# Reordering the last of four batches in a fused convolution-attention and channel-attention kernel

## The reference

```python
qkv = concat(x @ wq.T, x @ wk.T, x @ wv.T)                # 768 channels
dw  = depthwise 5x5 convolution of qkv
pw  = grouped 1x1 convolution of dw (groups of 8)
f   = concat(qkv, pw) as 64 heads of (query, key, value), 8 channels each
query, key = relu(query), relu(key)
scores = einsum("bhdn,bhen->bhde", concat(value, ones), key)
out = einsum("bhde,bhen->bhdn", scores, query)
out = out[:, :, :-1] / (out[:, :, -1:] + 1e-15)
x1 = batchnorm(proj @ out) + x
```

```python
norm = (x1 - mean) / sqrt(var + 1e-5)                     # over the positions of a channel
energy = (f_w @ norm + f_b).T @ (g_w @ norm + g_b)        # 1024 x 1024
attention = softmax(energy)
out = o_w @ ((h_w @ x1 + h_b) @ attention.T) + o_b + x1
```

## Time and profile before

| | us |
|---|---|
| median of 3 runs | 700.99 |
| the runs | 698.55, 703.51, 700.99 |
| span of the profiled execution, from its first to its last instruction | 700.8 |
| PE busy | 636.0 (91%) |
| DVE busy | 563.5 (80%) |
| POOL busy | 541.0 (77%) |
| ACT busy | 470.7 (67%) |

### The profile page before, as it was taken

One profiled execution on the slowest core, in us unless ns is written; L12 is line 12 of the kernel. 1 busy time (PEld: TensorE's weight loads), 2 busy tenths in 40 slices (PEclk: granted clock), 3 DMA queues, 4 the chain that ended last, 5 costly groups with the idle time before them and its releaser, 6 DMA issues.

```text
span 700.8 us, 8645 instructions
## 1 busy us (share of the span) xinstructions
PE 636.0 (91%) x3176; PEld 475.3 (68%) x3176; DVE 563.5 (80%) x661; ACT 470.7 (67%) x745; POOL 541.0 (77%) x253
## 2 busy tenths in 40 slices
PE   4979978999989999999989999999898977997998
PEld 3854537665868787656778877648677773485887
DVE  5899899788989999989999998989999993442321
ACT  4787608897777769888676977987886662232231
POOL 4899996999999899999999999999999891000000
PEclk9979999999999999999999999999999998899999
DMA  8000001001010000001100000000100000000000
GB/s 296 2 0 1 0 0 61 1 1 34 27 61 15 16 31 1 0 1 60 61 1 16 16 31 1 1 0 1 61 15 16 9 22 1 0 1 0 16 16 30
DMA packets 6537, 16.23 MB, mean 23 GB/s; under 512 B 864, under 2 KB 992, under 8 KB 5984
## 3 DMA queue, kind: packets, MB, share of 16 engines
q1 hardware_dynamic: 6496, 15.69, 6.3%
HBM read 11.50 MB, written 4.19 MB: 22 GB/s over the span
## 4 chain that ended last, share of the span: by engine, by line
PE 36%; issue 20%; DVE 16%; ACT 15%; POOL 12%; DMA 1%; POOLq 0%; SPq 0%; DVEq 0%; ACTq 0%
DVE ps L1143 9%; PE ps L629 7%; PE ps L605 7%; ACT prod L895 7%; POOL conv L1354 7%; POOL rows L1354 4%; PE ps L538 4%; PE ps L708 3%; DVE small L1280 2%; PE ps L471 2%; PE ps L620 2%; ACT raw L864 1%; PE ps L756 1%; PE ps L475 1%; PE ps L472 1%
## 5 line engine op out<-in xcount | busy, mean ns | idle before, releaser
L1354 POOL TENSOR_TENSOR conv<-conv,prod 128x930 f32<-128x930 f32 (+4 forms) x197 | 432.4, 2238 | 16.0 <-ACT prod L895 13.2
L1143 DVE SCALAR_TENSOR_TENSOR ps<-raw,dw_sb,ps 128x930 f32<-128x930 f32 (+4 forms) x295 | 354.1, 1201 | 7.6
L895 ACT ACTIVATE prod<-raw,dw_sb 128x930 f32<-128x930 f32 (+4 forms) x233 | 250.2, 1123 | 16.6 <-POOL conv L1354 16.6
L629 PE MATMUL ps<-ht,pt 128*128 128x256 f32 x512 | 115.4, 379 | 2.7 <-ACT pt L1050 2.7
L629 PEld LDWEIGHTS ps<-ht,pt 128*128 128x128 f32 x512 | 95.0, 190 | 14.8 <-ACT pt L1050 3.1
L1041 ACT ACTIVATE rows<-ps,small 128x1024 f32<-128x1024 f32 x32 | 35.6, 1113 | 82.2 <-DVE small L1284 82.2
L1354 POOL TENSOR_TENSOR rows<-rows,prod 128x930 f32<-128x930 f32 (+4 forms) x27 | 62.9, 2329 | 9.9 <-ACT prod L895 6.5
L1280 DVE TENSOR_REDUCE small<-ps 128x1 f32<-128x1024 f32 x32 | 39.1, 1220 | 27.9 <-PE ps L605 27.8
L605 PE MATMUL ps<-hi,t_hi 128*128 128x512 f32 x128 | 45.3, 436 | 14.4 <-ACT rows L1041 14.4
L471 PE MATMUL ps<-hi,wqkv_hi 128*128 128x512 f32 x92 | 38.9, 423 | 4.4 <-ACT vt L910 4.4
L605 PE MATMUL ps<-lo,t_hi 128*128 128x512 f32 x128 | 41.2, 404 | 0.0
(11 more groups left out here) (146 smaller groups left out, 1059.3 us busy)
## 6 DMA issues: line engine op xcount, KB each, us to landing
q_raw<-x_dram SPq DMA_DIRECT2D x8, 512.0 KB, 6.2
x<-x_dram SPq DMA_DIRECT2D x4, 1024.0 KB, 4.7
out_dram<-x_t SPq DMA_DIRECT2D x16, 256.0 KB, 2.3
conv<-wqkv_dram SPq DMA_DIRECT2D x1, 768.0 KB, 4.5
conv<-fg_dram SPq DMA_DIRECT2D x1, 512.0 KB, 5.1
proj_sb<-proj_dram SPq DMA_DIRECT2D x1, 512.0 KB, 7.6
pw_sb<-pw_dram SPq DMA_DIRECT2D x1, 384.0 KB, 6.1
mask_sb<-masks_dram SPq DMA_DIRECT2D x1, 264.0 KB, 6.2
```

The costliest lines, as they stand in the source:

```text
L629: mm = pe.matmul(dst[:, 0:C], pt[:, i % PT_BUFS, j, :], ht[:, j, :], start=(j == 0), stop=(j == NB - 1))
L895: act.activation(dst, view, ACT.Copy, scale=weight(t, i)).then_inc(prod_ready, 1)
L1143: return dve.scalar_tensor_tensor(dst, view, w, before, ALU.mult, ALU.add)
L1354: pool.tensor_tensor(total, total, product, ALU.add).then_inc(conv_pool, 1)
```

## The change

Only the last batch is changed; batches 0 to 2 run as before. It has these parts:

- The denominators are spread into four slots of the a kind (`last_spreads`, order h = 0, then 1) and DVE frees them (`last_scaled_queries`), so no spread uses a bank of the d kind.
- The projection is split (`projection_part`): the product with the raw queries of all four units comes directly behind `denominators`, with `fused_weights` in the middle; the product with the `pw` queries comes behind the spreads. Units 0 and 1 are in banks 4 and 5, units 2 and 3 in banks 6 and 7.
- DVE writes x1 to SBUF (`last_x1`), takes the statistics from there, and makes `lo` of a unit one unit later (`last_low`). ACT no longer copies x1; it only makes `hi`, from x1.
- ACT copies the fused weights before it adds the bias to the residual.
- The fold (`fold_spread` on PE, `fold_high` on ACT) comes ahead of the x1 transposes 2 and 3, and of the bias terms.
- Energies go alternately to banks 0, 1 and banks 6, 7, and wait for the exponential of the block two before.

```diff
-E_PAIR, T_PAIR = 0, 2
+E_PAIR, T_PAIR, ACC_PAIR = 0, 2, 6
...
-            a_end = lay_out(A_AT, [("mb_pw", 1)], b_, a_end)
+            a_end = lay_out(A_AT, [("mb_pw", 1), ("bc_pw", D_BC * (not nx))], b_, a_end)
...
-            d_end = lay_out(D_AT, [("sc_pw", 1), ("den_pw", 1), ("bc_pw", D_BC)], b_, d_end)
+            d_end = lay_out(D_AT, [("sc_pw", 1), ("den_pw", 1), ("bc_pw", D_BC * nx)], b_, d_end)
...
-            d_end = lay_out(D_AT, [("proj", D_PROJ), ("ht", D_HT // 2), ("fold", 1), ("ht2", D_HT // 2)], b_, d_end)
+            d_end = lay_out(D_AT, [("proj", proj_slots(b_)), ("ht", D_HT // 2), ("fold", 1), ("ht2", D_HT // 2)], b_, d_end)
...
+        def e_pair(b, i):
+            return ACC_PAIR if b + 1 == B and i % 2 else E_PAIR
+
+        def proj_bank(b, u):
+            if u < proj_slots(b):
+                return d_bank(D_AT["proj", b] + u)
+            return ps[:, ACC_PAIR + u - proj_slots(b), :]
...
+            def last_spreads(b):
+
+                slot, dens = A_AT["bc_pw", b], 2 * b + 2
+                pe.wait_ge(den_ready, dens)
+                for h in range(CK):
+                    banks = [a_slot(slot + CK * half + h) for half in range(2)]
+                    for i in range(2):
+                        if i == 1:
+                            pe.wait_ge(bc_part, CK * (dens - 1) + h + 1)
+                        for half in range(2):
+                            g = 2 * half + i
+                            mm = pe.matmul(banks[half][:, i * QUARTER:(i + 1) * QUARTER],
+                                           head_rows[HEADS * g:HEADS * (g + 1), h, :],
+                                           den[HEADS * g:HEADS * (g + 1), :], start=True, stop=True)
+                        if i == 0:
+                            mm.then_inc(bc_part, 1)
+                    mm.then_inc(a_full, 2)
+
+            def projection_part(b, u, kind):
+
+                c, h = UNITS[u]
+                if kind == 0 and u < proj_slots(b):
+                    d_slot(D_AT["proj", b] + u)
+                if kind == 1:
+                    pe.wait_ge(a_free, A_AT["bc_pw", b] + CK * (h + 1))
+                q = qp if kind else q_raw[:, b % 2]
+                for k in range(CK):
+                    mm = pe.matmul(proj_bank(b, u), mb[:, CK * kind + k, c * P:(c + 1) * P],
+                                   q[:, k, h * HALF:(h + 1) * HALF], start=(kind == 0 and k == 0),
+                                   stop=(kind == 1 and k == CK - 1))
+                if kind == 1:
+                    mm.then_inc(d_full if u < proj_slots(b) else last_proj_full, 1)
+
+            def last_front(b):
+
+                denominators(D_AT["den_pw", b], D_AT["sc_pw", b], qp, A_AT["pwq", b] + A_PWQ)
+                for u in range(CK):
+                    projection_part(b, D_PROJ - 1 - u, 0)
+                fused_weights(A_AT["mb_pw", b], A_AT["st_pw", b], 1)
+                for u in range(CK, D_PROJ):
+                    projection_part(b, D_PROJ - 1 - u, 0)
+                last_spreads(b)
+                pe.wait_ge(a_free, A_AT["mb_pw", b] + 1)
+                for u in range(D_PROJ):
+                    projection_part(b, u, 1)
+
             def energy(b, i):
 
-                if i > 0:
-                    pe.wait_ge(exp_done, NB * b + i)
+                buffers = 1 if b + 1 < B else 2
+                if i >= buffers:
+                    pe.wait_ge(exp_done, NB * b + i - buffers + 1)
+                if i == 1 and buffers == 2:
+                    pe.wait_ge(last_x1_lo, D_PROJ)
...
-                        mm = pe.matmul(ps[:, E_PAIR + h, :], lhs, m[:, h * HALF:(h + 1) * HALF],
+                        mm = pe.matmul(ps[:, e_pair(b, i) + h, :], lhs, m[:, h * HALF:(h + 1) * HALF],
...
+                else:
+                    last_front(b)
...
                 x1_transposes(b, 1)
-                x1_transposes(b, 2)
-                if with_next:
+                if with_next:
+                    x1_transposes(b, 2)
                     fused_weights(A_AT["mb_raw", b + 1], A_AT["st_raw", b + 1], 0)
                 output_weights(b, 1)
+                if not with_next:
+                    fold_spread(b)
+                    x1_transposes(b, 2)
                 x1_transposes(b, 3)
...
+                if not with_next:
+                    fused_weights(A_AT["mb_pw", b], 1)
                 act.wait_ge(res_loaded, 16 * (b + 1))
...
+                    else:
+                        act.activation(hi[:, c, cols], x1[:, c, cols], ACT.Copy).then_inc(x1_hi, 1)
...
                 x1_transposes(b, 1)
+                if not with_next:
+                    fold_high(b)
                 x1_transposes(b, 2)
...
+            def last_scaled_queries(b):
+
+                slot = A_AT["bc_pw", b]
+                for h in range(2):
+                    cols = slice(h * HALF, (h + 1) * HALF)
+                    dve.wait_ge(a_full, slot + 2 * CK)
+                    for t in range(CK):
+                        dve.tensor_tensor(qp[:, t, cols], qp[:, t, cols], a_bank(slot + CK * h + t),
+                                          ALU.mult).then_inc(a_free, 1)
+
+            def last_x1(b):
+
+                for u, (c, h) in enumerate(UNITS):
+                    cols = slice(h * HALF, (h + 1) * HALF)
+                    bank, slots = proj_bank(b, u), proj_slots(b)
+                    if u < slots:
+                        dve.wait_ge(d_full, D_AT["proj", b] + u + 1)
+                    else:
+                        dve.wait_ge(last_proj_full, u - slots + 1)
+                    dve.scalar_tensor_tensor(x1[:, c, cols], bank, bn_scale[:, c:c + 1], x1[:, c, cols],
+                                             ALU.mult, ALU.add).then_inc(x1_ready, 1)
+                    dve.wait_ge(x1_ready, D_PROJ * b + u + 1)
+                    op = dve.bn_stats(stats[:, c, h, :], x1[:, c, cols])
+                    if h == 1:
+                        step(op)
+                        step(dve.bn_aggr(mv[:, c, :], stats[:, c, :, :]))
+                        dve.tensor_scalar(stat_ve[:, c:c + 1], mv[:, c, 1:2], NORM_EPS, None,
+                                          ALU.add).then_inc(var_ready, 1)
+                    elif u < slots:
+                        op.then_inc(d_free, 1)
+                    if u >= 1:
+                        last_low(b, u - 1)
+                last_low(b, D_PROJ - 1)
+
+            def last_low(b, u):
+
+                c, h = UNITS[u]
+                cols = slice(h * HALF, (h + 1) * HALF)
+                dve.wait_ge(x1_hi, D_PROJ * b + u + 1)
+                dve.tensor_tensor(lo[:, c, cols], x1[:, c, cols], hi[:, c, cols].bitcast(F32),
+                                  ALU.subtract).then_inc(last_x1_lo, 1)
```

100 lines of the change are left out of this document (58 added, 42 removed).

## The result

The changed kernel took 683.14 us (median of four executions, 681.15 to 687.99) against 702.25 us for the kernel before beside it (four, 698.55 to 704.79): a ratio of 0.975, 95% interval 0.971 to 0.979. With two repeats (medians 684.89 and 684.44) there are 16 executions of the changed kernel, mean 684.6, and 51 of the kernel before, mean 701.8. That is a gain of 17.2 us, and twice the standard error of the two means leaves 15.9 to 18.4.

What follows compares the result with a forecast made beforehand. TensorE, busy 636 of 700.8 us, was taken as the bound, with waits and a halved clock bare in the last batch. Gains of 6.9 and 6.9 make 13.8 us, forecasting 687.2 us; range 683.8 to 691.0.

Steps and rivals of the forecast that it cites:

- the sum: Last batch: 6.9 us gained in the front plus 6.9 in the energies, 13.8 us off the span of 700.8.
- the front: Last batch up to the transform, 40.60 us before; gain 8.2 us if the clock holds, 6.9 with one fall.
- the energies: Last batch's first two energies up to values 0, 17.24 us before; values 0 would start 6.9 us earlier.
- the rival in which vector becomes slower: Behind the projection: vector becomes the front's bound, adding 2.0 us behind unit 0; 689.2 us; chance 0.08.
- So I count one fall: Behind the spreads, from about 597: one clock fall costing 1.9 us of TensorE's time, 1.3 after slack; chance 0.50.
- The first rival: The clock holds through the spreads: gain 15.1 us, 685.9 us on the median's scale; chance 0.22.
- The rival of a longer low stretch: 1.2 GHz from the first spread well into the projection, costing 3.3 us: gain 11.8, 689.2 us; chance 0.13.
- Some 0.6 of it is slack: Ahead of the fold: 0.6 of the fall's 1.9 us is absorbed, because TensorE no longer waits for ht.
- the clean front: The front without a clock fall: transform starts at 616.2 instead of 624.45, 8.2 us gained.
- of which 1.9 is the fall that goes with the gap: Energy 1: closing the gap ahead of it also removes a half-clock stretch, 1.9 of the energies' 6.9 us.
- Without it the second spread would wait for the copy: ScalarE's copy of the fused weights must precede its residual passes, or the second spread waits; the swap costs nothing.
- The fold's reordering: Vector's and ScalarE's fold chain, bare from 620.4 to 622.84 before, would lie beside the transposes and bias terms.

Runs made afterwards that it cites:

- act_copy: The changed kernel with ScalarE copying x1 from the bank again and vector scaling and adding into the bank; 689.98 us, 0.985 of the kernel before.
- after_third: The changed kernel, unedited, run once more as a repeat; 684.44 us, 0.976 of the kernel before.
- raw_around: The changed kernel with the raw half of units 1 and 0 between the spreads and the other half; 681.89 us, 0.972 of the kernel before.
- ht_early: raw_around with one ht moved ahead of the last two lo on vector; 680.19 us, 0.971 of the kernel before.

## Why the prediction was right, and where it was wrong

**The mechanism was right, and the number too small.** The gain lies in the two stages that the sum names, 8.2 us in the front's mean (6.9 in the sum) and 7.7 in the energies' (6.9); the other two stood still, and the steps read as written: raw passes directly behind the denominators, one wait for the multiplies, 0.44 us of wait ahead of the fold, statistics directly behind the scale-and-add, energies without a gap. The pieces of vector that could not be read came out as taken (0.75 us for the scale-and-add, 0.77 in the sum; 0.03 for its own write, 0.04 in the sum), so the rival in which vector becomes slower did not come. Each half alone gave its own part. act_copy confirmed vector's chain by undoing it.

**The step "So I count one fall" was wrong as a certainty and right as a mean.** The price put on it was 1.3 us; seven profiles of this gap show 0 three times and 1.41, 1.69, 1.69 and 3.05, in the mean 1.12. The first rival, the clock that holds, is what the first profile shows. The rival of a longer low stretch, priced at 3.3 us above a clock that holds, came out near in its amount, 3.05 in after_third, but by another path: it had 2.0 of it in the spreads, which took 2.34 us there as in every profile of this gap, and the whole fall lay in the projection. These were not competing forecasts but three outcomes of one kernel, and the time is a mean over them.

**"Some 0.6 of it is slack" was wrong.** Every us of the fall came through to the front: other half and front grew alike, to 0.01 us, and the 0.44 ahead of the fold was there in all three profiles of the changed kernel. The slack was TensorE's wait for vector; but vector works on the units that these passes fill, and in the changed kernel's chain of waits it works without a wait from unit 1 to ht (596.11 to 604.23). A fall within the first eight passes, which unit 1 needs, moves both.

**Two terms of the clean front were mis-sized.** I had 8.2 us of gain if the clock holds; it is 8.98. The spreads were 2 x 1.46 = 2.9; the four in one piece took 2.34, so eight more passes cost 0.88, and about 0.6 of the 1.46 for x8 in the earlier trace rows is a part that one piece has only once; what it consists of was not tried. That is 0.6. The fold started 25.14 us after the front's begin instead of 25.65, mostly this shortening, and from there to the transform it took 6.48 instead of 6.7.

**What made the gain 3.4 us larger than the sum, term by term.** The old front costs 40.95 in the mean instead of the 40.60 of the profile (0.35). The old energies cost 18.07 instead of 17.08 (0.99). The new front is 32.74 in the mean instead of 33.7 (0.96). The new energies are 10.55 in the windows instead of 10.34 (-0.21: the first transposes of rows, behind the wait for exp 0, took 1.09 us instead of 0.87). That makes 2.1; 1.3 are not placed. The largest term is the energies of the kernel before: "of which 1.9 is the fall that goes with the gap" took the clock of one execution for its usual price. Energy 1 took 4.62 us there and energy 2 ran at full clock; in the second and third profile energies 1 and 2 both ran partly at 1.2 GHz (two of their passes took 1.05 us there instead of 0.62).

**The range** was built on the scatter of three runs and on cases of the change alone. It left out that the profiled execution of before is itself one draw, at the mild end in the stages that the change removes.

**"Without it the second spread would wait for the copy" was wrong**, and touched no number. ScalarE has nothing to do from 579.8 to 585.3, and the residual is long there.

**The fold's reordering was valued too high.** I counted the chain from 620.4 to 622.84 as bare; of it 0.76 us was, and 0.3 net of the wait for ht that comes instead. The sum was not hurt, since it was built forward from TensorE's work and not from what is removed.

**The page on the clock.** The Trainium skill ("TensorE: Matmul & The Clock Gate", HAM oscillation) has idle gaps bring the clock down. By that rule I said that 1.3 us would not cost it. The traces agree in three profiles of seven and contradict it in four, at a gap of 1.48 us behind 2.34 us of matmuls with 32 rows. Where the same narrow matmuls had full-width passes on both sides and no gap (raw_around, ht_early), the clock held in both profiles.

## What to carry to other kernels

When part of a stage's work needs none of the waits in front of it, put it on both sides of the small work that waits, not only ahead of it: behind the small work it hides the consumer's latency too, which was worth 1.5 us here. In the two profiles with this order the clock held too, which is too few to count on.

Before pricing a removal by a stretch of low clock in one profile, look at the same stretch in another execution. If a gap sometimes costs the clock, put its mean cost in the sum and its worst in the range, for the kernel before as well as for the one after. Slack in front of a wait absorbs a delay only if what the engine waits for doesn't come through the same delay.

Compare stages, not spans. A span difference of 20.3 us held 4.7 from a part of the program that the change doesn't touch.

## What was not expected of the hardware

The granted clock is not a function of the program alone. The same instructions had TensorE busy between 528.1 and 533.7 us ahead of the last batch, and the same 1.48 us gap gave other-half times of 7.11, 8.52, 8.80 and 10.16 us. The profiles don't show what decides it.

GpSimd's reciprocal square root of a 128x1 tile took 0.55 us in every batch of the kernel before and in batches 0 to 2 of the changed one, and 0.93 in the last batch of the changed one. ht_early has both in one batch. GpSimd's and vector's timeline there:

```profile
595.85 0.93 POOL L1481 TENSOR_TENSOR small<-small 128x1 f32<-128x1 f32 x1 [23.10 <-DVE small L1309]
598.27 0.55 POOL L1481 TENSOR_TENSOR small<-small 128x1 f32<-128x1 f32 x1 [1.50 <-DVE small L1309]
```

```profile
595.69 0.68 DVE L1321 TENSOR_TENSOR lo<-x,hi 128x512 fp32r<-128x512 f32 x1
598.11 0.68 DVE L1373 TENSOR_TENSOR ht<-ps,oh_b 128x512 f32<-128x512 f32 x1
```

The long one runs beside a vector operation with both inputs in SBUF (lo from `x` and `hi`), the short one beside one that reads a bank (ht). It fits all the others: where GpSimd took 0.55, vector's lo read the bank (`lo<-ps,hi`), and where it took 0.93, `x`. That the shared access to SBUF is the reason was not tried apart.

It is off the path, under vector's lo, and cost nothing here. The spread into banks of its own was not tried apart from the order in which the raw half stands.
